# Splitting all weights on VectorE, and writing dense weights over expert weights block by block

## The chip, the cores and the metric

The kernel runs on one core of a Trainium2 chip. The metric is the device time of one execution, in microseconds (us). A core has five engines, each with a queue of its own that it works off in order: TensorE (PE: matmuls, with PEld for its weight loads), VectorE (DVE), ScalarE (ACT), GpSimd (POOL) and SyncE (SP, which issues DMAs). Engines wait for one another through semaphores only.

## What is computed

A two-layer "macaron" network on x of shape (4, 256, 256), that is 1024 tokens of width 256. `_L0_ffn` is a mixture of 16 experts of width 176 (4 per token) with a shared expert of width 704; `_L1_ffn` is a mixture of 32 experts of width 96 (up to 8 per token), which the kernel computes densely for all tokens; `_L0_attn` is an attention with 16 heads; `_L1_attn` is a state-space layer.

```python
x = L0_attn_x
x = x + 0.5 * _L0_ffn_ref(_layernorm(x), ...)
x = x + _L0_attn_ref(_layernorm(x), ...)
x = x + 0.5 * _L0_ffn_ref(_layernorm(x), ...)
x = x + 0.5 * _L1_ffn_ref(_layernorm(x), ...)
x = x + _L1_attn_ref(_layernorm(x), ...)
x = x + 0.5 * _L1_ffn_ref(_layernorm(x), ...)
```

All inputs are float32. The kernel multiplies in float16 and keeps the precision by splitting each operand into a high half and a low half (`whi` and `wlo` of the weights, `xhi` and `xlo` of the input, `hhi` and `hlo` of the hidden layer) and adding three products: high by high, high by low, low by high.

## The kernel before

The 1024 tokens are two halves of 512. The feed-forward work is twelve passes (`PASSES`), numbered p0 to p11: a shared pass of 6 units (SH: p0, p2, p4, p6), a routed pass of 16 units (RT: p1, p3, p5, p7), each for one half and one of the two uses of `_L0_ffn`, and four dense passes of 24 units (F1: p8 to p11). A unit is `gate` and `up` (matmuls into PSUM), `tanh` (ScalarE), `act` (VectorE), `h` (VectorE), `hi` (ScalarE), `lo` (GpSimd, `hh` or `hp` minus its high half) and `down` (matmuls). A routed unit handles two blocks of 128 token slots, each block of one expert; the tokens are scattered to DRAM by `send` (GpSimd, indirect DMA), loaded transposed by `load_xs` (SyncE), the result goes through `turn`, `hT_copy`, `y_copy` and `store_y`, and is gathered back by `gather` (GpSimd) and `combine` (VectorE, L1475). A dense unit has one more VectorE step, `fac` (L1330), that multiplies by the routing factor of each token.

The order of the work is written out by hand: `make_threads` makes lists ("threads") of pieces for each engine, and the strings in `ORDER` say how the threads of one engine are merged, one letter a thread and a number for how many pieces. In the VectorE string `m` is `act`, `h` and `fac`, `w` the weights' low halves, `c` `combine`, `r` the routing, `A` to `D` the layer norm. The strings decide what stands in front of what on an engine; the waits in each `piece` decide when it runs.

Weights come in pieces through a ring of 12 slots (`SLOTS`) in the tile `stage`. The first `NW0` = 40 pieces are 6 shared ones (768 columns), 32 half experts (608 columns) and 2 of the attention (768); `load_w0` loads piece g into slot g % 12 once the low half of piece g - 12 is made. The 28 chunks of the dense stage and the state-space layer (`WCH1`, 768 columns) follow as pieces 40 to 67: `load_w1`. Each piece is split like this: ScalarE writes `whi` = 256 x stage as float16 (`w0_hi` L851, `w1_hi` L864). Then either VectorE makes `wlo` = 256 x stage - `whi` in one `scalar_tensor_tensor` (L1387; pieces 0 to 5 and the even ones up to 38, 23 in all), or ScalarE scales the stage in place (`w0_scale` L854, `w1_scale` L868) and GpSimd subtracts (`w0_lo` L766, `w1_lo` L771): the 17 odd pieces 7 to 39 and all 28 chunks.

The tiles `whi` and `wlo` hold shared weights, attention weights and experts; the dense chunks are written over them. Chunk 0 waits until the last shared pass (p6) is done, chunk 8 (`EXP0 // CW`), the first that reaches into expert columns, until the last routed pass (p7) is done:

```python
if n == 0:
    act.wait_ge(down_done, UNIT[6] + NSH)
if n == EXP0 // CW:
    act.wait_ge(down_done, UNIT[7] + NRT)
```

In the order of before, ScalarE has `w1_hi` 0 to 7 within p7 and 8 to 27 within the first 14 units of p8; GpSimd has `w1_lo` 0 to 7 after units 5 to 11 of p7, and 8 to 27 after units 1 to 21 of p8. Unit c of p8 waits for chunk c, the state-space layer's `proj` for chunk 27. Unit c of p1 waits for the experts up to 2c + 1 (`wait_expert`).

## Time and profile before

| | us |
|---|---|
| median of 3 runs | 994.18 |
| lowest, highest | 990.6, 996.01 |
| the profiled execution, its time | 983.99 |
| its span, first to last instruction | 982.2 |
| its mean granted clock of TensorE | 0.959 of full speed |

The profile is of one execution. Its page gives the busy time of each engine, the span in 40 slices and the costliest groups of instructions; the other views give busy time in chosen stretches, groups by line, and the instructions in order of time. "Idle before, released by" stands in square brackets behind an instruction in the timeline. Busy time is not the same as time on the path that sets the end.

### The profile page before, as it was taken

How to read it: one execution, taken by the hardware profiler on the slowest of the kernel's cores; microseconds unless marked ns; L12 is line 12 of the kernel's file. 1: busy time of each engine (PE TensorE's matmuls, PEld its weight loads, DVE VectorE, ACT ScalarE, POOL GpSimd, SP SyncE). 2: the span in 40 equal slices, each digit the busy share in tenths (PEclk: the TensorE clock that was granted, in tenths of full speed). 3: DMA queues.
4: the chain of work that ended last, by engine and by line, in shares of the span. 5: the costliest groups of instructions: out<-in, count | busy, mean ns of one | idle time of the engine just before them, and what ended most of it. 6: DMA issues, size and time to landing. Idle time of an engine off the chain costs nothing.

```text
span 982.2 us, 20723 instructions
## 1 busy us (share of the span) xinstructions
PE 855.6 (87%) x6872; PEld 557.1 (57%) x6872; DVE 712.4 (73%) x1392; ACT 500.0 (51%) x929; POOL 477.3 (49%) x464
## 2 busy tenths in 40 slices
PE   2767788999748899788889897899999899999997
PEld 1356666777424667647675554454566445665564
DVE  6897326988778888736447987888978777785554
ACT  2867553688515677536767852345333543333332
POOL 3865278424667344288825866532443224432322
PEclk9979999999559999999999998999999999999999
DMA  8796546632122224847965522111110211112221
GB/s 303 287 219 154 138 146 123 135 85 59 60 65 78 64 55 102 254 153 154 195 166 167 166 100 68 47 54 47 51 57 23 76 51 47 54 41 92 73 68 65
DMA packets 123267, 106.62 MB, mean 109 GB/s; under 512 B 75672, under 2 KB 97944, under 8 KB 123168
## 3 DMA queue, kind: packets, MB, share of 16 engines
q1 hardware_dynamic: 117024, 88.51, 32.1%
q0 software_dynamic: 6144, 16.79, 6.0%
q8 instruction: 62, 1.02, 0.4%
q14 instruction: 37, 0.30, 0.1%
HBM read 58.98 MB, written 30.02 MB: 91 GB/s over the span
## 4 chain that ended last, share of the span: by engine, by line
PE 60%; issue 7%; DVE 6%; POOL 3%; ACT 2%; DMA 2%; SPq 1%; POOLq 0%; DVEq 0%; ACTq 0%
PE ps L1063 24%; PE ps L1110 12%; PE ps L1038 7%; PE ps L1092 5%; PE ps L1254 2%; PE ps L1078 1%; PE ps L1177 1%; PE ps L1216 1%; PE ps L1211 1%; PE ps L1285 1%; DVE hid L1330 1%; DVE hid L1324 1%; POOL back L760 1%; PE ps L1274 1%; POOL xs_dram L745 1%
## 5 line engine op out<-in xcount | busy, mean ns | idle before, releaser
L717 POOL TENSOR_TENSOR hh<-hid,hh 128x512 f16<-128x512 f32 x120 | 143.5, 1198 | 238.7 <-ACT hh L829 238.4
L1324 DVE SCALAR_TENSOR_TENSOR hid<-gtanh,ps 128x512 f32<-128x512 f32 (+2 forms) x184 | 114.4, 622 | 160.4 <-ACT gtanh L808 145.8
L1063 PE MATMUL ps<-xhi,whi 128*128 128x512 f16 x480 | 186.8, 389 | 24.4 <-DVE hid L1324 20.1
L808 ACT ACTIVATE gtanh<-ps 128x512 f32<-128x512 f32 (+2 forms) x184 | 100.4, 545 | 204.7 <-PE ps L1063 169.3
L1063 PE MATMUL ps<-xlo,whi 128*128 128x512 f16 x480 | 186.5, 388 | 0.0
L1063 PE MATMUL ps<-xhi,wlo 128*128 128x512 f16 x480 | 186.1, 388 | 0.0
L1110 PE MATMUL ps<-whi,hh 128*128 128x256 f16 x960 | 174.5, 273 | 5.2 <-POOL hh L717 5.2
L1038 PE MATMUL ps<-whi,xs_sb 128*128 x992 | 130.5, 245 | 34.1 <-issue 23.6
L1338 DVE SCALAR_TENSOR_TENSOR hid<-hid,ps 128x512 f32<-128x512 f32 (+2 forms) x184 | 114.6, 623 | 28.9 <-PE ps L1038 12.2
L1110 PE MATMUL ps<-wlo,hh 128*128 128x256 f16 x480 | 131.0, 273 | 0.0
L829 ACT ACTIVATE hh<-hid 128x512 f16<-128x512 f32 x120 | 75.1, 626 | 95.1 <-DVE hid L1330 64.8
L1038 PE MATMUL ps<-wlo,xs_sb 128*128 x496 | 118.0, 242 | 0.0
L1110 PEld LDWEIGHTS ps<-whi,hh 128*128 128x128 f16 x960 | 94.1, 98 | 30.3 <-issue 5.9
L1038 PEld LDWEIGHTS ps<-whi,xs_sb 128*128 128x128 f16 x992 | 71.7, 99 | 55.9 <-issue 44.0
L714 POOL TENSOR_TENSOR hp<-hid,hp 128x352 f16<-128x352 f32 x64 | 57.0, 892 | 94.7 <-ACT hp L819 94.5
L1063 PEld LDWEIGHTS ps<-xhi,whi 128*128 128x128 f16 x480 | 47.8, 100 | 80.0 <-issue 33.1
L1330 DVE TENSOR_TENSOR hid<-hid,xs_sb 128x512 f32<-128x512 f32 x96 | 84.3, 878 | 9.8 <-DMA xs_sb<-c_dram 7.5
L1063 PEld LDWEIGHTS ps<-xhi,wlo 128*128 128x128 f16 x480 | 47.9, 100 | 59.8 <-issue 5.5
L745 POOL DMA_INDIRECT xs_dram<-xr,pos x64 | 65.9, 1030 | 28.3 <-issue 26.5
L1092 PE MATMUL ps<-whi,hh 128*128 x372 | 75.2, 282 | 4.4 <-ACT hh L836 3.7
L760 POOL DMA_INDIRECT back<-ys_dram,pos x64 | 68.5, 1070 | 16.4 <-issue 14.7
L1063 PEld LDWEIGHTS ps<-xlo,whi 128*128 128x128 f16 x480 | 47.8, 100 | 44.5 <-issue 3.9
(208 smaller groups left out, 1587.4 us busy)
## 6 DMA issues: line engine op xcount, KB each, us to landing
ys_dram<-y_sb SPq DMA_DIRECT2D x60, 256.0 KB, 2.5
xs_sb<-c_dram SPq DMA_DIRECT2D x64, 192.0 KB, 2.7
scr<-w_in SPq DMA_DIRECT2D x28, 384.0 KB, 4.9
scr<-we_in SPq DMA_DIRECT2D x32, 304.0 KB, 4.6
xs_sb<-c_dram SPq DMA_DIRECT2D x64, 128.0 KB, 2.9
xs_sb<-c_dram SPq DMA_DIRECT2D x64, 64.0 KB, 2.7
xs_dram<-y_sb SPq DMA_DIRECT2D x1, 3968.0 KB, 15.0
scr<-ws_in SPq DMA_DIRECT2D x8, 384.0 KB, 7.1
```

Source lines behind the costliest of these rows:

```text
L717: pool.tensor_tensor(hlo[:, k, :], hid[:, k % 2, :], hhi[:, k, :], ALU.subtract).then_inc(lo_done, 1)
L745: pool.indirect_dma_start(out=xs_dram, out_offset=bass.IndirectOffsetOnAxis(ap=pos[:, h, j, i:i + 1], axis=0), in_=xr[:, i, :], in_offset= ...
L760: pool.indirect_dma_start(out=back[:, slot, :], out_offset=None, in_=ys_dram[h], in_offset=bass.IndirectOffsetOnAxis(ap=pos[:, h, j, t:t + ...
L808: act.activation(gtanh[:, n % 2, 0:w], ps[:, G_BANK, 0:w], ACT.Tanh, scale=0.5 / W_SCALE)\
L829: act.activation(hhi[:, k, :], hid[:, k % 2, :], ACT.Copy).then_inc(hi_done, 1)
L1038: mm = pe.matmul(ps[:, bank, j * I0:(j + 1) * I0], xs_sb[:, slot + j, a + kc, :], w[:, ds(offset[k + j] + (EXP0 + kc * 2 * I0 + part), I0) ...
L1063: mm = pe.matmul(ps[:, bank, :], w[:, off:off + P], a[:, kc, t0:t0 + HN], start=(i == 0), stop=(i == 3 * KC - 1))
L1092: mm = pe.matmul(ps[:, Y_BANK + m % 2, D * b:D * b + D], hh[0:wide, k, at_h:at_h + P], w[0:wide, ds(offset[2 * (n % REGS) + b] + (EXP0 + 2 ...
L1110: mm = pe.matmul(acc[:, i, :], a[:, k, i * P:(i + 1) * P], w[:, off:off + D], start=(c == 0 and i % 2 == 0 and m == 0), stop=(c == NUM[r] ...
L1324: dve.scalar_tensor_tensor(out=hid[:, k, 0:w], in0=gtanh[:, k, 0:w], scalar=1.0, in1=ps[:, G_BANK, 0:w], op0=ALU.add, op1=ALU.mult).then_i ...
L1330: dve.tensor_tensor(hid[:, n % 2, :], hid[:, n % 2, :], fac[:, m % FRING, :], ALU.mult).then_inc(fac_done, 1)
L1338: dve.scalar_tensor_tensor(out=hid[:, k, 0:w], in0=hid[:, k, 0:w], scalar=scale, in1=ps[:, U_BANK, 0:w], op0=ALU.mult, op1=ALU.mult).then_ ...
```

## The change

All 45 pieces that GpSimd split are split by VectorE, with the same fused instruction as the others; the scalings of the stage on ScalarE and the subtractions on GpSimd go. A helper `w_split` names the semaphore and count of a piece, and every waiter uses it, `load_w0` and `load_w1` on SyncE among them. A dense chunk n that reaches into expert columns waits for only as many routed units of p7 as can still use these experts (`chunk_free`: an expert has at most four blocks, so block b is never of an expert below b // 4; chunk 9 waits for 4 units, 12 for 8, 15 for 12, 19 and later ones for 16). The lower bound of the expert's offset in `gate` says the same to the compiler. The strings of `ORDER` are written anew for all five engines.

```diff
@@ -220,7 +220,7 @@
         put("ACT", "w", "w0_hi", g)
-        if g < NSH or g % 2 == 0:
+        if g < NW0:
             put("DVE", "w", "w0_lo", g)
@@ -231,8 +231,7 @@
         put("ACT", "w", "w1_hi", j)
-        put("ACT", "w", "w1_scale", j)
-        put("POOL", "w", "w1_lo", j)
+        put("DVE", "w", "w1_lo", j)
@@ -560,13 +559,20 @@
-            return g < NSH or g % 2 == 0
+            return True
 
         def lo_count(g):
 
-            if g >= NW0:
-                return lo_count(NW0 - 1) + g - NW0 + 1
             return sum(piece_on_dve(i) == piece_on_dve(g) for i in range(g + 1))
+
+        def w_split(g):
+
+            return (w_lo_dve if piece_on_dve(g) else w_lo_pool), lo_count(g)
+
+        def chunk_free(n):
+
+            last = ((n + 1) * CW - 1 - EXP0) // EW
+            return (HN // P) * (last + 1) // 2
@@ -683,7 +686,7 @@
                     if n >= SLOTS:
-                        sp_.wait_ge(w_lo_pool, lo_count(g - SLOTS))
+                        sp_.wait_ge(*w_split(g - SLOTS))
@@ -764,11 +767,6 @@
-                elif name == "w1_lo":
-                    g = NW0 + n
-                    pool.wait_ge(w_scaled, lo_count(g))
-                    pool.tensor_tensor(wlo[:, n * CW:(n + 1) * CW], stage[:, g % SLOTS, :], whi[:, n * CW:(n + 1) * CW],
-                                       ALU.subtract).then_inc(w_lo_pool, 1)
@@ -859,14 +857,10 @@
-                    if n == EXP0 // CW:
-                        act.wait_ge(down_done, UNIT[7] + NRT)
+                    if n >= EXP0 // CW:
+                        act.wait_ge(down_done, UNIT[7] + min(NRT, chunk_free(n)))
...
-                elif name == "w1_scale":
-                    g = NW0 + n
-                    act.activation(stage[:, g % SLOTS, :], stage[:, g % SLOTS, :], ACT.Copy, scale=W_SCALE)\
-                        .then_inc(w_scaled, 1)
@@ -1022,7 +1016,8 @@
-                            offset[k + j] = pe.snap(at_expert[k + j], min_val=0, max_val=(E0 - 1) * EW)
+                            offset[k + j] = pe.snap(at_expert[k + j], min_val=(2 * c + j) // (HN // P) * EW,
+                                                        max_val=(E0 - 1) * EW)
@@ -1387,6 +1382,12 @@
+                elif name == "w1_lo":
+                    g = NW0 + n
+                    dve.wait_ge(w_hi, g + 1)
+                    dve.scalar_tensor_tensor(out=wlo[:, n * CW:(n + 1) * CW], in0=stage[:, g % SLOTS, :], scalar=W_SCALE,
+                                             in1=whi[:, n * CW:(n + 1) * CW], op0=ALU.mult, op1=ALU.subtract)\
+                        .then_inc(w_lo_dve, 1)
```

The new strings, read out as pieces:

| engine | before | after |
|---|---|---|
| PE | second half's `logits` before the gate of p1, unit 0; its `rank` before unit 3 | `logits` after the gate of p1, unit 11; `rank` after the gate of unit 12 |
| DVE | 13 of its 23 `wlo` pieces by the end of p0; routing of the second half within units 0 to 3 | pieces 0 to 19 before `act` of p1, unit 0; 20 to 36 before `h` of unit 5; routing of the second half in units 11 to 13 |
| DVE | no dense piece | `w1_lo` 0 to 15 behind `h` of p7, units 4 to 15; 16 to 21 behind p8, units 0 to 8; 22 to 27 from p8, unit 20 to p9, unit 1 |
| ACT | `w1_hi` 0 to 7 in p7 | `w1_hi` 0 to 15 in p7, chunk 12 behind the `y_copy` of unit 9; 16 to 27 in p8, units 0 to 6 |
| POOL | `send` of the first half with three `lo` and one `wlo` between | the same with two `lo` and no `wlo` between |
| SP | `load_w0` 0 to 22, then the first transposed load | `load_w0` 0 to 25, then the first three transposed loads |

## Rows read from the trace of the kernel before

**Rows 1.** The page: TensorE in 40 slices; the DMA view: transposed loads, us to landing.

```profile
PE   2767788999748899788889897899999899999997
...
xs_sb<-xs_dram SPq DMA_TRANSPOSE x124, 3.4
```

**Rows 2.** Busy time by stage: us, busy (count) per engine, clock, DMA share, GB/s.

```profile
20.00:62.60 42.60, 25.73 (x156) 13.30 (x156) 36.66 (x42) 29.66 (x48) 33.26 (x29) 0.92 0.82 281
62.60:90.00 27.40, 22.86 (x240) 20.13 (x241) 23.97 (x57) 22.15 (x44) 18.13 (x14) 0.88 0.83 180
90.00:135.00 45.00, 35.25 (x373) 28.58 (x373) 16.18 (x40) 24.55 (x56) 17.72 (x19) 0.96 0.52 134
...
450.00:515.00 65.00, 55.13 (x633) 45.05 (x631) 33.65 (x96) 46.22 (x95) 39.88 (x40) 1.00 0.76 174
515.00:650.00 135.00, 119.62 (x740) 70.03 (x738) 109.56 (x165) 66.97 (x109) 86.47 (x72) 0.96 0.34 105
650.00:982.00 332.00, 322.55 (x1971) 187.84 (x1970) 242.28 (x411) 122.92 (x205) 106.30 (x97) 0.99 0.18 57
```

**Rows 3.** Timeline, DVE, POOL, PE, 49 to 63 us: start, duration, idle before.

```profile
49.11 8.31 DVE L1387 SCALAR_TENSOR_TENSOR wlo<-scr,whi 128x608 f16<-128x608 f32 x1
...
50.44 3.94 POOL L766 TENSOR_TENSOR wlo<-scr,whi 128x608 f16<-128x608 f32 x3
...
60.71 0.19 PE L1146 MATMUL ps<-rwhi,xhi 128*128 128x32 f16 x1 [8.03 <-issue]
...
62.63 0.47 PE L1038 MATMUL ps<-whi,xs_sb 128*128 x2 [0.91 <-issue]
```

**Rows 4.** Timeline, POOL, DVE, PE, 594 to 604 us.

```profile
594.52 1.17 POOL L717 TENSOR_TENSOR hh<-hid,hh 128x512 f16<-128x512 f32 x1
...
598.35 3.22 POOL L771 TENSOR_TENSOR wlo<-scr,whi 128x768 f16<-128x768 f32 x2
...
594.79 7.07 DVE L1475 SCALAR_TENSOR_TENSOR x<-back,wk,x 128x256 f32<-128x256 f32 x1 [0.78 <-DMA back<-ys_dram,pos]
...
603.20 0.58 PE L1063 MATMUL ps<-xhi,whi 128*128 128x512 f16 x1 [5.46 <-DVE hid L1324]
```

**Rows 5.** Dense stage by shape, 515 to 650 us: busy us, mean ns, idle before.

```profile
L1330 DVE TENSOR_TENSOR hid<-hid,xs_sb 128x512 f32<-128x512 f32 x27 | 34.3, 1271 | 3.3 <-DMA xs_sb<-c_dram 2.6
...
L1475 DVE SCALAR_TENSOR_TENSOR x<-back,wk,x 128x256 f32<-128x256 f32 x16 | 19.3, 1234 | 0.8 <-DMA back<-ys_dram,pos 0.8
L1324 DVE SCALAR_TENSOR_TENSOR hid<-gtanh,ps 128x512 f32<-128x512 f32 x28 | 19.1, 684 | 13.9 <-ACT gtanh L808 13.7
```

**Rows 6.** Weight lines: ns min/median/max, first and last start, forms.

```profile
L1387 DVE SCALAR_TENSOR_TENSOR wlo<-scr,whi x23: 779/951/8315, 21.9 to 98.3; 128x608 f16<-128x608 f32 x16, 128x768 f16<-128x768 f32 x7
...
L766 POOL TENSOR_TENSOR wlo<-scr,whi x17: 1325/1357/1880, 41.5 to 105.9; 128x608 f16<-128x608 f32 x16, 128x768 f16<-128x768 f32 x1
...
L771 POOL TENSOR_TENSOR wlo<-scr,whi x28: 1627/1646/2080, 472.6 to 625.0; 128x768 f16<-128x768 f32 x28
...
L868 ACT ACTIVATE scr<-scr x28: 826/832/845, 455.3 to 581.5; 128x768 f32<-128x768 f32 x28
```

**Rows 7.** Timeline, POOL scatters of the first half (first, last), SP.

```profile
21.05 1.25 POOL L745 DMA_INDIRECT xs_dram<-xr,pos  x1 [5.37 <-issue]
...
46.98 1.04 POOL L745 DMA_INDIRECT xs_dram<-xr,pos  x1 [0.30 <-issue]
...
50.27 2.62 SPq L650 DMA_TRANSPOSE xs_sb<-xs_dram  x2
```

**Rows 8.** A routed block on TensorE: the chain at 176 us; timeline at 89.65 us.

```profile
178.57 0.91 PE ps L1038 x12
179.48 1.09 PE ps L1092 x10
...
182.53 0.33 PE ps L1078 x6
...
89.65 0.32 PE L1038 MATMUL ps<-whi,xs_sb 128*128 x2 [1.60 <-DVE wlo L1387]
```

More of the change, by code:

```diff
@@ L1006, in wait_shared @@
             def wait_shared(j):
-                pe.wait_ge(w_lo_dve, lo_count(j))
+                pe.wait_ge(*w_split(j))
             def wait_expert(e):
-                pe.wait_ge(w_lo_dve, lo_count(NSH + 2 * e))
-                pe.wait_ge(w_lo_pool, lo_count(NSH + 2 * e + 1))
+                pe.wait_ge(*w_split(NSH + 2 * e))
+                pe.wait_ge(*w_split(NSH + 2 * e + 1))
             def piece(name, n):
```

19 lines of the change are left out of this document (8 added, 11 removed), and 98 rows, old and new, of the table ORDER.

## The prediction

> **What bounds the kernel now.** I read the page first, then the busy time stage by stage, then the waits, and last the timeline of each engine around the gaps of TensorE. TensorE's slices are near nine tenths in most of the span [rows 1]; they show where it isn't at work: at the start, and twice in the middle. The stages put numbers on it [rows 2]. TensorE is idle for 42.6 - 25.73 = 16.9 us from 20 to 62.6 us (shared pass 0 and the first expert weights), 4.5 us to 90 us (first half of routed pass 1), 9.8 us to 135 us, 9.9 us from 450 to 515 us (routed pass 7), and 15.4 us from 515 to 650 us (dense pass 8, while the dense weights are still being split). After 650 us, when no weight is left to split, only 9.4 of 332 us are idle. So the time is TensorE's work plus its gaps, and a change to VectorE, ScalarE or GpSimd counts only where it closes or opens a gap.
>
> The gaps have one cause in common. A VectorE instruction with both inputs in SBUF that starts beside a run of GpSimd subtractions does not end before the run does. At 49.11 us the low half of an expert piece takes 8.31 us while GpSimd works off `hh` and `wlo` subtractions; TensorE, whose next instruction is the router's logits (they need a VectorE result queued behind), stands for 8.03 us [rows 3]. At 594.79 us one `combine` takes 7.07 us: GpSimd began a run of `hh` and `wlo` subtractions at 594.52 us and ended it at 601.57 us; TensorE's matmuls wait 5.46 us and start again at 0.58 us each, the slow rate [rows 4]. By shape, `fac` (L1330) has a mean of 1.27 us in this stage, where L1324, as wide but with an input in PSUM, has 0.684; `combine` (L1475), half as wide, has 1.23 us [rows 5]. The instructions that read PSUM do not stretch. That is 27 x (1.271 - 0.684) + 16 x (1.234 - 0.684) = 24.6 us of VectorE time at least, lost in this stage.
>
> **The change, part by part.** Removed: 17 + 28 = 45 GpSimd subtractions of 1.36 and 1.65 us (23.1 + 46.1 = 69 us), and 45 ScalarE scalings of about 0.7 and 0.83 us (L868 has the row of the wider; some 35 us). Added: 45 fused VectorE instructions, of which the 23 there are show the price: 16 at best 0.78 us for a 608-wide piece, 7 are 768 wide and take about the median of 0.95 us. That is 16 x 0.78 + 29 x 0.95 = 40.0 us [rows 6]. The price is known; the question is only what it stands beside.
>
> *Start, to 135 us.* The part that sets the first routed block is the scatter of the tokens: 16 indirect DMAs on GpSimd from 21.05 to 48.02 us, with three `lo` and one `wlo` subtraction between them, then the transposed loads, issued at 50.27 us and taking 2.62 us to issue [rows 7]. The new order takes out one `lo` (1.17 us [rows 4]) and the `wlo` (1.36 us [rows 6]): scatters end at 45.5 us, the pair of transposes is issued by 45.5 + 2.25 + 2.62 = 50.4 us, and lands 3.4 us later [rows 1], at 53.8 us. In the new order the gate of block 0 of pass 1 follows the shared pass at once and the logits of the second half come eleven blocks later, so the 8.03 us stall has nothing to stand on. VectorE must have made pieces 0 to 19 and twelve `act` and `h` by then: 6 x 0.95 + 14 x 0.78 + 12 x 0.684 = 25 us from 22 us on, plus some 4 us (an estimate: six small steps at most as long as an `act` each) for block table and layer norm: 51 us. I put the first routed gate at 55 us, a little behind the landing, in place of 62.63 [rows 3]: 7.6 us gained (bounds 3, if VectorE has all its pieces 5 us late, and 9, if it lands at once). Next, blocks 0 to 5 of pass 1. They take 89.65 - 62.63 = 27.0 us [rows 3, 8]. TensorE needs 2 x 0.91 + 1.09 + 0.33 = 3.24 us a block, 19.4 us for six. VectorE in the new order has 18 pieces there and twelve narrower `act` and `h`: 18 x 0.78 + 12 x at most 0.684 = 22.2 us, and about 2 us for the shared output's add. VectorE is the later one: 24 us, 3 us gained (bounds: loss of 3, gain of 7). From 90 to 135 us the y stores and the transposes set the pace and stay: 0 (-3 to +3). Start: 10.6 us gained.
>
> *New waits.* `w1_hi` from chunk 9 on waits for a number of routed blocks in place of all 16. Behind it on ScalarE stand `tanh`, `hi` and `y_copy` of later blocks, and TensorE behind these. But each such wait stands after a `y_copy` that waits for the same block or a later one (chunk 12 asks for 8 blocks and follows `y_copy` of the tenth), so it costs nothing. On SyncE `load_w0` and `load_w1` now wait for VectorE's pieces; behind them stand transposed loads and y stores. The piece waited for is 12 back: cover of several us, and if it is gone, each late piece costs TensorE its 0.78 to 0.95 us. Cost 0 (0 to 4).
>
> *Pass 7, 450 to 515 us.* VectorE gets 16 pieces, 15.2 us, and is busy 33.7 of 65 us now; ScalarE changes 8 scalings for 8 or 9 `w1_hi` of about the same length; GpSimd loses 13 us [rows 2, 6]. VectorE would be at 49 of 65 us, so it doesn't bind, but a piece in front of an `act` delays the chain gate, `tanh`, `act`, `up`, `h` of a block. Bounds: nothing, or half of the pieces on the path, 8 us, or a gain of 3 for transposes of `h` that wait less for GpSimd. I take a loss of 2.
>
> *Pass 8, 515 to 650 us.* VectorE gets the other 12 pieces (11.4 us) and loses the 24.6 us of stretching: 109.6 - 24.6 + 11.4 = 96 of 135 us [rows 2, 5, 6], so it is less loaded than before with more to do. What is left on GpSimd is one `lo` of 1.17 us [rows 4] per block, and there are 28 blocks in 135 us [rows 5], so a stretch ends after at most that. Of 15.4 us idle and some 4 us of slow clock (119.6 us busy at a granted clock of 0.96 in place of 1.00 [rows 2]) I leave 4 us for the routing and the factor loads: 15 us gained (bounds 6 and 19).
>
> Other stages hold no changed instruction, only another order: 0 (-5 to +5).
>
> Sum against the profiled execution (span 982.2, 983.99 us): -10.6 + 0 + 2 - 15 = -23.6, so 960.4 us. The runs shown have a median of 994.18, 10.2 us more than the profiled one; I take the difference over: 970.6 us.
>
> How a stretch ends can be set against a page. The stretched `combine` spans four GpSimd instructions [rows 4]. The Trainium skill, page "SBUF — State Buffer", section "SBUF: two separate sides", says that whichever engine starts first has the shared ports for its one whole instruction. By that, a stretch is at most one subtraction, 1.65 us, and the new VectorE instructions, with two SBUF inputs, would hold up GpSimd's `lo` in turn. The trace shows the run, not the one instruction, as the unit, so the rule alone undersells what goes away.
>
> **Rivals.** *VectorE is late.* In pass 1 and pass 7 it takes its upper costs: the six blocks get 3 us longer in place of 3 shorter, pass 7 loses 8 in place of 2. Then the sum is -7.6 + 3 + 8 - 15 = -11.6: 982.6 us. For it: its work per block in pass 1 is above TensorE's. Against: the stage from 90 us leaves VectorE idle for 29 of 45 us [rows 2], so a delay there is made good.
>
> *An overlap costs one instruction's length only.* The removed pieces then explain 1.65 of the 8.03 us and 1.65 of the 5.46 us, 0.2 to 0.3 of a gap. With 0.3 of the 25.6 us gained, less 2: -5.7, 988.5 us. Against: the `combine` and the run of four subtractions end within 0.3 us of each other [rows 4]. The rule of that page would end here.
>
> *More closes than I count.* All bounds of the gain together are 17 us more; some two thirds of that, because GpSimd's `lo` and ScalarE are free earlier: 960 us.
>
> *The gap only changes its owner*: TensorE waits for the y stores, the scatters and the routing of the second half, and the end stays, 994 us. For it: the start is full of such transfers (DMA share 0.82 and 0.83 [rows 2]).
>
> *Slower.* VectorE's pieces lie on the path in all three stages. Place: between `act` and `h` of one block, where the new order puts up to three pieces. Price: 40.0 us if each piece delays TensorE by its length, less the 25.6 recovered: +14.4, 1008.6 us. It decides once more than 25.6 of the 40 us, two pieces in three, lie on the path; against it, VectorE has 24 us of work to TensorE's 19.4 in six blocks of pass 1, and room in passes 7 and 8.
>
> **How the numbers follow.** Forecast 0.55 (970.6 us), VectorE late 0.13 (982.6), one instruction only 0.07 (988.5), more closes 0.10 (960), gap changes owner 0.08 (994), slower 0.07 (1008.6). The range leaves out the last two, and takes in the rest with some room below for the bounds of the unchanged stages: 954 to 988 us. A measurement of this kernel tells about 0.5% from no change, 5 us: below 989.2 is faster, 0.82 (of the one-instruction case about half); within, 0.11; above 999.2, 0.07.
>
> **What would show it.** Right: no GpSimd `wlo`; L1330 and L1475 near 0.69 and 0.5 us on average; first routed gate near 55 us; TensorE idle under 6 us in pass 8; first dense chunk beyond the eighth split before the last routed block. Wrong: VectorE's `wlo` as the releaser of TensorE's waits in pass 1 or 7; `fac` still stretched beside single `lo`; a new gap at the routing of the second half.

## The result, and the profile after

| | before | after |
|---|---|---|
| median of the runs, us | 993.52 (990.6 to 996.01, 4 runs) | 951.08 (944.98 to 952.91, 4 runs) |
| profiled execution, us (span) | 983.99 (982.2) | 952.91 (951.1) |
| granted clock of that execution | 0.959 | 0.973 |

The ratio is 0.9563, 95% interval 0.9509 to 0.9617: 43 us faster. Forecast were 970.6 us and a range of 954 to 988 us; 951.08 lies below it. The direction was right, the size was not: 43 us where 23.6 were summed.

The first view of after is the busy time by stage, as in [rows 2]: the start, pass 1 up to 79 us (its block 6 begins on TensorE at 81.27 us), the rest of pass 1, pass 7, pass 8, and the rest. Columns are us, busy us (instructions) of PE, PEld, DVE, ACT, POOL, then clock, DMA share and GB/s.

```profile
20.00:55.60 35.60, 28.09 (x155) 15.62 (x156) 27.15 (x41) 25.91 (x42) 25.23 (x22) 0.95 0.84 313
55.60:79.00 23.40, 17.73 (x201) 14.14 (x199) 19.78 (x36) 16.83 (x34) 6.24 (x6) 1.00 1.07 252
79.00:128.00 49.00, 40.08 (x455) 31.60 (x454) 26.69 (x81) 26.24 (x59) 18.19 (x19) 1.00 0.55 131
...
438.00:508.00 70.00, 58.47 (x639) 46.09 (x637) 50.12 (x112) 47.35 (x97) 28.09 (x32) 0.98 0.86 197
508.00:603.00 95.00, 94.96 (x620) 57.84 (x619) 80.23 (x145) 40.11 (x70) 48.47 (x43) 1.00 0.39 114
603.00:951.00 348.00, 340.06 (x2085) 199.32 (x2083) 259.45 (x444) 129.59 (x215) 116.03 (x105) 1.00 0.19 57
```

In pass 8 TensorE is busy for 94.96 of 95.00 us at a clock of 1.00. It has no gap left. At the start there is still one (28.09 of 35.60 us), and in pass 7 another (58.47 of 70).

The same pass of before, cut at its own ends, shows what its 117.5 us were made of: 15.4 us idle (117.50 - 102.12), and 7.0 us by which TensorE was busy longer than the 95.16 us that after needs for the same matmuls.

```profile
516.20:633.70 117.50, 102.12 (x632) 59.36 (x630) 97.07 (x134) 60.94 (x98) 79.58 (x63) 0.96 0.35 108
```

The lower clock is only a part of these 7.0 us. The granted clock was 0.72 from 566 to 572 us and 0.66 from 600 to 610 us, behind the two long gaps, and 1.00 elsewhere: 0.28 x 6 + 0.34 x 10 = 5.1 us at most, gaps included. What the other 2 us are no row shows.

The shapes of pass 8 on VectorE answer to [rows 5] (busy us, mean ns, idle before):

```profile
L1325 DVE TENSOR_TENSOR hid<-hid,xs_sb 128x512 f32<-128x512 f32 x24 | 19.9, 830 | 0.8
...
L1388 DVE SCALAR_TENSOR_TENSOR wlo<-scr,whi 128x768 f16<-128x768 f32 x12 | 14.1, 1183 | 0.0
L1476 DVE SCALAR_TENSOR_TENSOR x<-back,wk,x 128x256 f32<-128x256 f32 x16 | 7.7, 532 | 0.0
```

`fac` fell from a mean of 1.271 to 0.830 us, `combine` from 1.234 to 0.532. The new pieces of VectorE cost what the old ones did (minimum, median, maximum in ns, first and last start), none of them above 2 us:

```profile
L1382 DVE SCALAR_TENSOR_TENSOR wlo<-scr,whi x40: 778/784/1744, 21.8 to 95.4; 128x608 f16<-128x608 f32 x32, 128x768 f16<-128x768 f32 x8
...
L1388 DVE SCALAR_TENSOR_TENSOR wlo<-scr,whi x28: 944/951/1926, 455.7 to 606.9; 128x768 f16<-128x768 f32 x28
```

At the start, the timeline answers to [rows 3, 7]: the last of the first half's scatters on GpSimd, the transposed loads on SyncE's queue, the first gate of pass 1 on TensorE, which waited for nothing.

```profile
44.10 0.98 POOL L748 DMA_INDIRECT xs_dram<-xr,pos  x1 [0.31 <-issue]
...
47.63 7.86 SPq L653 DMA_TRANSPOSE xs_sb<-xs_dram  x6
...
54.53 0.31 PE L1033 MATMUL ps<-whi,xs_sb 128*128 x2
```

To see where the 31 us between the two profiled executions are, take the first `tanh` of each pass on ScalarE as its begin:

```
begin of          before   after   lead
pass 1              64.6    55.6    9.0
pass 2             137.3   128.0    9.2
pass 7             449.1   438.0   11.1
pass 8             516.2   507.7    8.5
pass 9             633.7   602.9   30.8
end                982.2   951.1   31.1
```

Pass 8 gave 22.3 us, the start 9, and all the rest nothing on balance. Blocks 0 to 5 of pass 1 gave next to nothing: block 6 begins on TensorE at 81.27 us, 26.7 us behind the first gate, where before took 27.0, and what it waited for is a VectorE piece:

```profile
81.27 0.32 PE L1033 MATMUL ps<-whi,xs_sb 128*128 x2 [0.76 <-DVE wlo L1382]
```

The medians differ by 12 us more than these two executions do; that is a question of its own below.

### The profile page after: what moved, and what is told of

It reads as the page before. It is cut to its first block, busy times and chain, and to the rows that moved or that the text cites. A ratio compares the mean times of both kernels' runs of the same rounds, so it can differ in the third digit from the quotient of the medians.

```text
span 951.1 us, 20697 instructions
## 1 busy us (share of the span) xinstructions
PE 845.6 (89%) x6872; PEld 554.0 (58%) x6872; DVE 704.3 (74%) x1437; ACT 469.5 (49%) x884; POOL 416.1 (44%) x419
## 4 chain that ended last, share of the span: by engine, by line
PE 73%; issue 7%; DVE 5%; POOL 4%; DMA 4%; another core or an unknown queue 2%; SPq 2%; ACT 2%; POOLq 0%; DVEq 0%; ACTq 0%
PE ps L1058 29%; PE ps L1105 15%; PE ps L1033 10%; PE ps L1087 6%; POOL xs_dram L748 3%; PE ps L1249 2%; PE ps L1073 2%; PE ps L1172 2%; DMA xs_dram<-y_sb 2%; DMA scr<-we_in 1%; PE ps L1211 1%; PE ps L1206 1%; PE ps L1280 1%; SPq L653 1%
## 5 line engine op out<-in xcount | busy, mean ns | idle before, releaser
L1105 PE MATMUL ps<-whi,hh 128*128 128x256 f16 x960 | 176.8, 275 | 7.2 <-POOL hh L720 7.2
L717 POOL TENSOR_TENSOR hp<-hid,hp 128x352 f16<-128x352 f32 x64 | 59.6, 932 | 125.7 <-ACT hp L817 125.4
L1325 DVE TENSOR_TENSOR hid<-hid,xs_sb 128x512 f32<-128x512 f32 x96 | 71.6, 746 | 5.5 <-DMA xs_sb<-c_dram 3.0
L1087 PE MATMUL ps<-whi,hh 128*128 x372 | 72.5, 275 | 2.6 <-ACT hh L834 2.5
## 6 DMA issues: line engine op xcount, KB each, us to landing
xs_sb<-c_dram SPq DMA_DIRECT2D x64, 128.0 KB
```

The source lines that it names most:

```text
L1087: mm = pe.matmul(ps[:, Y_BANK + m % 2, D * b:D * b + D], hh[0:wide, k, at_h:at_h + P], w[0:wide, ds(offset[2 * (n % REGS) + b] + (EXP0 + 2 ...
L1105: mm = pe.matmul(acc[:, i, :], a[:, k, i * P:(i + 1) * P], w[:, off:off + D], start=(c == 0 and i % 2 == 0 and m == 0), stop=(c == NUM[r] ...
L1325: dve.tensor_tensor(hid[:, n % 2, :], hid[:, n % 2, :], fac[:, m % FRING, :], ALU.mult).then_inc(fac_done, 1)
```

## The experiments

Blocks are named pass.block. Each run has its own runs of the kernel before on the same chip, so ratios can be compared from chip to chip (after: 0.956) and microseconds of pass 8 and of the start too (pass 9 took 123.0 to 123.4 us in every profile); the lengths of pass 1 and of passes 2 to 6 only on one chip.

### Does GpSimd's subtraction make pass 8 long?

Twenty subtractions are put back beside the changed kernel, as ballast. In the next three runs the ballast lies on scratch columns that, as it turned out, hold the head constants of the last stage, so that stage computes with overwritten constants; its instructions are the same.

```diff
   pool.tensor_tensor(hlo[:, k, :], hid[:, k % 2, :], hhi[:, k, :], ALU.subtract).then_inc(lo_done, 1)
+  for _ in range({1: 1, 2: 1, 4: 1, 5: 1, 7: 1, 9: 1, 10: 1, 11: 1, 12: 1, 13: 1, 14: 1, 16: 1, 17: 2,
+                  18: 1, 19: 2, 20: 2, 21: 1}.get(c, 0) if r == F1_PASSES[0] else 0):
...
+      pool.tensor_tensor(scr[:, 10368 + 384 * (k % 4):10752 + 384 * (k % 4)].bitcast(F16),
+                         scr[:, 9216:9984], scr[:, 9984:10368].bitcast(F16), ALU.subtract)
```

> The changed kernel with 20 more GpSimd subtractions in pass 8, each 768 wide (float32 minus float16 into float16, as the removed ones of the dense chunks), on scratch columns that nobody reads, behind the lo of the blocks where the kernel before had its own. No engine waits for them; they change nothing of the output. Theory (GpSimd's reads stretch VectorE's instructions with two SBUF inputs, and that was the time of pass 8): fac in pass 8 goes from a mean of 0.75 us back to 1.1 to 1.3 us, pass 8 from 95.2 to 103 to 115 us, the whole to 959 to 971 us. Rival 1 (pass 8 gained from the dense weights being written early, or from ScalarE's removed scalings): fac may stretch, but pass 8 stays within 2 us of 95.2 and the whole at 951. Rival 2 (an overlap costs one instruction's length only): fac near 0.95 us, pass 8 at most 97 us.

Measured: pass 8 took 113.5 us (+18.3), the ratio is 0.9703 (0.9671 to 0.9734). On that chip the kernel before took 982.37 us and passes 2 to 6 were shorter in every profile, so the whole, 951.63 us, says less than pass 8 does; by its ratio it is 14 us longer than after. VectorE and TensorE in pass 8:

```profile
L1333 DVE TENSOR_TENSOR hid<-hid,xs_sb 128x512 f32<-128x512 f32 x24 | 30.0, 1252 | 0.8
...
L1341 DVE SCALAR_TENSOR_TENSOR hid<-hid,ps 128x512 f32<-128x512 f32 x24 | 16.4, 685 | 0.7
L1327 DVE SCALAR_TENSOR_TENSOR hid<-gtanh,ps 128x512 f32<-128x512 f32 x24 | 16.3, 679 | 9.9 <-POOL hh L721 8.8 <-ACT gtanh L814 1.1
...
PE ps L1066 <- DVE hid L1327: 12.7, 10, 2.4
```

`fac` is back at 1.252 us, the two that read PSUM stay at 0.685 and 0.679, and TensorE waits ten times for `act` (L1327). But see what `act` itself waited for: 8.8 us for GpSimd's `hh` (L721), the `lo` that the ballast had pushed back (3.4 us in after). `combine` is not back: a mean of 0.568 us, where before had 1.234. So two mechanisms work here, the stretch and GpSimd's own lateness.

The same ballast in five runs of four:

```diff
-  for _ in range({1: 1, 2: 1, 4: 1, 5: 1, 7: 1, 9: 1, 10: 1, 11: 1, 12: 1, 13: 1, 14: 1, 16: 1, 17: 2,
-                  18: 1, 19: 2, 20: 2, 21: 1}.get(c, 0) if r == F1_PASSES[0] else 0):
+  for _ in range({3: 4, 7: 4, 11: 4, 15: 4, 19: 4}.get(c, 0) if r == F1_PASSES[0] else 0):
```

> The same 20 subtractions, but in five runs of four, behind the lo of blocks 3, 7, 11, 15 and 19 of pass 8. If a VectorE instruction stays blocked to the end of a run of back-to-back GpSimd instructions, single fac or combine of 5 to 8 us appear, about one a run, TensorE stands about 4 us at each, and pass 8 gets 15 to 25 us longer (110 to 120 us), more than with the same work laid singly. If only one instruction's length is lost at a time, no fac is longer than 1.6 + 0.7 = 2.3 us or so and pass 8 is no longer than with single ones. If nothing of this is on the path, 95 us.

Measured: pass 8 at 122.8 us (+27.6), ratio 0.9809 (0.9768 to 0.985). The same work in runs costs 9 us more than laid singly. One `fac` was shut out for the whole run; in another run a `wlo` was not (timeline, DVE and POOL):

```profile
550.46 7.62 DVE L1333 TENSOR_TENSOR hid<-hid,xs_sb 128x512 f32<-128x512 f32 x1
...
551.11 6.42 POOL L728 TENSOR_TENSOR scr<-scr 128x768 f16<-128x768 f32 x4
...
509.01 2.40 DVE L1396 SCALAR_TENSOR_TENSOR wlo<-scr,whi 128x768 f16<-128x768 f32 x1
...
506.82 7.69 POOL L728 TENSOR_TENSOR scr<-scr 128x768 f16<-128x768 f32 x4
```

`fac` ended at 558.08 us, 0.55 us behind the end of the run at 557.53. The `wlo` that began at 509.01 us, in the middle of the other run, ended at 511.41, while that run went on to 514.51; there GpSimd paid, 7.69 us for four in place of 6.42. The five runs took 7.69, 7.27, 6.42, 6.95 and 8.05 us, so the run that shut VectorE out is the shortest. Forecast were about five such long stops; there was one, and pass 8 is longer than forecast all the same, since GpSimd's `lo` stands behind each run as well.

The control: GpSimd writes but reads nothing.

```diff
-      pool.tensor_tensor(scr[:, 10368 + 384 * (k % 4):10752 + 384 * (k % 4)].bitcast(F16),
-                         scr[:, 9216:9984], scr[:, 9984:10368].bitcast(F16), ALU.subtract)
+      pool.memset(scr[:, 9216 + 768 * (k % 4):9984 + 768 * (k % 4)].bitcast(F16), 0.0)
```

> The changed kernel with 20 GpSimd memsets of 1536 float16 columns in the places of the 20 subtractions: GpSimd writes SBUF but reads nothing. If it is GpSimd's reading that stretches VectorE, fac stays at 0.75 us and pass 8 at 95 us. If any GpSimd work does (or if it only matters that GpSimd's own lo comes later), fac and pass 8 move as with the subtractions, in proportion to the memsets' own length, which no row shows yet.

```profile
L1333 DVE TENSOR_TENSOR hid<-hid,xs_sb 128x512 f32<-128x512 f32 x24 | 17.9, 746 | 0.8
...
L728 POOL MEMSET scr<- 128x1536 f16 x20 | 27.4, 1379 | 0.0
```

`fac` is not stretched (0.746 us) beside 27.4 us of memsets, yet pass 8 takes 101.3 us (+6.1), and `act` waits 6.6 us for GpSimd's `hh`. That is mostly the second mechanism, but not alone: some VectorE instructions with one SBUF tensor as input are held up by memsets. One that takes 0.18 us in the changed kernel took 2.60 us, to the end of a run of two (timeline, DVE and POOL):

```profile
565.69 2.60 DVE L1505 TENSOR_SCALAR active<-cum 128x28 f32<-128x28 f32 x1
...
565.56 2.69 POOL L728 MEMSET scr<- 128x1536 f16 x2
```

Of the 18.3 us of the subtractions, then, at most some 6 to 7 are GpSimd's lateness (the memsets are 1.38 us long, the subtractions 1.61 at their fastest) and some 11 to 12 the stretch. This split is an estimate; it takes the two to add up.

ScalarE's removed scalings, put back as ballast (scratch columns that no stage uses):

```diff
   act.activation(whi[:, n * CW:(n + 1) * CW], stage[:, g % SLOTS, :], ACT.Copy, scale=W_SCALE).then_inc(w_hi, 1)
+  act.activation(scr[:, s:s + 6 * P].rearrange("p (a b) -> p a b", b=P),
+                 ident.unsqueeze(1).to_broadcast([P, 6, P]), ACT.Copy, scale=W_SCALE)
```

> The changed kernel with 45 more ScalarE copies with a scale, of 640 and 768 columns, one behind the high half of each piece that had a scaling before; they read a constant and write scratch columns that nobody reads, and nobody waits for them. They test the rival that the removed 35 us of ScalarE work were part of the gain. Expected: at most 0.8 us at a few blocks of pass 1 and pass 7, pass 8 at 95 to 97 us, the whole within 4 us of the changed kernel (ratio to before 0.955 to 0.960). If the scalings mattered: 4 us or more.

Measured: 953.94 us, ratio 0.9621 (0.9575 to 0.9668). Pass 8 took 98.6 us, +3.3 where at most 1.8 were expected, and pass 2 began at 129.4 us (126.9 and 128.0 in the two profiles of after). The whole is some 6 us longer by its ratio, where at most 4 were expected; with two runs the intervals still overlap. So ScalarE's part of the split is a term too, which the prediction had set to nothing, and every gain of "moved work" below has it inside.

### Undoing one part, doing one part

Dense chunks back on ScalarE and GpSimd, behind the same blocks, with the early writing kept:

```diff
-        put("DVE", "w", "w1_lo", j)
+        put("ACT", "w", "w1_scale", j)
+        put("POOL", "w", "w1_lo", j)
```

> One part of the change undone: the 28 dense chunks have their low halves from ScalarE's scaling and a GpSimd subtraction again, behind the same blocks as VectorE's pieces stand now; the expert pieces stay on VectorE, and the early writing of the dense weights stays. Theory: the start keeps its gain (first block of pass 6 within 2 us of 409), pass 8 is 10 to 18 us longer than 95.2, pass 7 within 3 us, and the whole is 962 to 972 us. If the early writing is what made pass 8 shorter, the whole stays within 3 us of 951.

Measured: ratio 0.9661 (0.9631 to 0.9691), pass 8 at 105.2 us (+10.0, the low edge of what was expected), pass 7 at 71.3, the start as in after (pass 1 at 56.2 us). Pass 8 held 13 of these subtractions, not 20: the early writing had put the others into pass 7.

Odd expert pieces back on GpSimd, in the new order:

```diff
-        if g < NW0:
+        if g < NSH or g % 2 == 0:
             put("DVE", "w", "w0_lo", g)
```

> Another part undone: the 17 odd expert and attention pieces have their low halves from ScalarE's scaling and a GpSimd subtraction again, in the new order, behind the same blocks; the dense chunks stay on VectorE. If these subtractions delayed the scatters and stretched VectorE at the start, the first block of pass 1 moves from 55.6 to between 58 and 65 us and the whole is 3 to 9 us longer than the changed kernel. If the start's gain came from the new order alone (logits of the second half eleven blocks later), the first block of pass 1 stays at 55 to 57 us and the whole within 2 us. Pass 8 stays at 95 us in both cases.

Measured: ratio 0.9694 (0.9643 to 0.9745). On one chip with `after_again`, pass 1 began at 62.4 us in place of 55.7 and pass 2 at 139.8 in place of 126.9: 12.8 us, more than the 9 expected; from there on nothing (the ends differ by 13.3), and pass 8 was 95.2 us. TensorE waited for GpSimd, and VectorE was held up beside `hh` and two `wlo` (waits of TensorE from 20 to 140 us: us, times, longest; timeline of DVE and POOL):

```profile
PE ps L1031 <- POOL wlo L767: 8.4, 4, 3.2
...
38.34 4.78 DVE L1380 SCALAR_TENSOR_TENSOR wlo<-scr,whi 128x608 f16<-128x608 f32 x1
...
39.81 2.65 POOL L767 TENSOR_TENSOR wlo<-scr,whi 128x608 f16<-128x608 f32 x2
```

Late writing again, once in an order close to that of before, once laid out evenly:

```diff
-                        act.wait_ge(down_done, UNIT[7] + min(NRT, chunk_free(n)))
+                        act.wait_ge(down_done, UNIT[7] + NRT)
```

> The third part undone: chunks 8 to 27 of the dense weights are written only after the last routed block of pass 7, as in the kernel before, with ScalarE's, VectorE's and SyncE's orders moved accordingly; all low halves stay on VectorE. Theory (pass 8 gained from GpSimd's missing subtractions): 20 pieces of 0.95 us stand in pass 8 in place of 12, VectorE has room, pass 7 gets up to 3 us shorter and pass 8 up to 4 us longer: whole within 3 us of the changed kernel. Rival (the early writing is the gain): pass 8 at 108 to 118 us, the whole 12 to 20 us longer.

> The changed kernel with chunks 8 to 27 written only after pass 7 once more, but laid out one a block: in the run before, two VectorE pieces stood ahead of a block's act and waited 3.6 us for ScalarE, which cost pass 8 5.8 us at one block; that was the order and not the late writing. Here ScalarE's part of a chunk comes four blocks and VectorE's three blocks ahead of its use. Theory (early writing is worth little by itself once GpSimd has no subtractions): pass 8 at 95 to 99 us, the whole within 4 us of the changed kernel. Rival (late writing costs in any order): pass 8 at 104 us or more.

Measured: ratios 0.9692 (0.9633 to 0.9751) and 0.9653 (0.9602 to 0.9704); pass 8 at 106.7 and 102.5 us, pass 7 at 70.9 and 71.0. Neither side's figures came out: theory had pass 8 at most at 99 us, the rival at 108 and at 104 us or more. The theory that late writing costs nothing once GpSimd is free is wrong: in the better of two layouts it costs 7.3 us of pass 8. Twenty pieces then stand in a pass in which TensorE needs 3.9 us a block and VectorE was busy for 80 of 95 us with twelve. An order tuned for it might do better; 7.3 us is an upper bound.

One part alone, in the order of before. First the dense chunks:

```diff
-        put("ACT", "w", "w1_scale", j)
-        put("POOL", "w", "w1_lo", j)
+        put("DVE", "w", "w1_lo", j)
```

> The kernel before with one part of the change alone: the 28 dense chunks have their low halves from one fused VectorE instruction, behind the same blocks where GpSimd had them; no early writing, every other order as before, expert pieces still half on GpSimd. Theory (the subtractions on GpSimd were what pass 8 lost): pass 8 goes from 117.5 to 98 to 104 us, pass 7 within 2 us, the whole 12 to 20 us faster than before. Rival, after the run with late writes (106.7 us in pass 8 with all low halves on VectorE): the early writing is worth 11 us of its own, so pass 8 stays at 106 us or more and the whole gains 11 us or less.

Then the odd expert pieces:

```diff
-            return g < NSH or g % 2 == 0
+            return g < NW0
```

> The kernel before with only the 17 odd expert and attention pieces moved from GpSimd to VectorE, each behind its even neighbour; all other orders as before (the logits of the second half still stand early in pass 1), dense chunks still on GpSimd. If the subtractions themselves cost the start (stretching and late scatters), the first block of pass 1 goes from 64.7 to 56 to 60 us, pass 2 begins 8 to 13 us earlier, and the whole is 6 to 13 us faster than before. If the gain needs the new order, the first block of pass 1 stays above 62 us and the whole gains 3 us or less; if VectorE is then late in pass 1, pass 1 gets longer than 75 us and it may be slower.

Measured: ratios of 0.9936 (0.9917 to 0.9956) for the chunks and 0.9983 (0.9952 to 1.0013) for the expert pieces. The chunks alone gave 6.3 us where 12 to 20 were expected, the expert pieces nothing. Undone, the same parts cost 10 and 13 us by their ratios. In pass 8 with the chunks on VectorE (111.4 us) the rows show who is late now (waits: us, times, longest):

```profile
PE ps L1049 <- DVE hid L1310: 9.9, 5, 2.7
PEld ps L1049 <- DVE wlo L1379: 8.9, 4, 3.1
```

And at the start, with the expert pieces on VectorE, the 8.03 us stall of [rows 3] is 2.56 us long, but it ends no earlier (62.03 us, 60.71 in [rows 3]). VectorE, which owes the logits their operand, itself stood for ScalarE's high half before (timelines of TensorE and of VectorE):

```profile
62.03 0.18 PE L1143 MATMUL ps<-rwhi,xhi 128*128 128x32 f16 x1 [2.56 <-issue]
63.93 0.32 PE L1035 MATMUL ps<-whi,xs_sb 128*128 x2 [0.95 <-issue]
```

```profile
57.96 0.79 DVE L1384 SCALAR_TENSOR_TENSOR wlo<-scr,whi 128x608 f16<-128x608 f32 x1 [2.96 <-ACT whi L848]
```

### The corners: moved work without the order, order without the moved work

The kernel before with all 45 pieces on VectorE, every order and wait as it was:

```diff
-            return g < NSH or g % 2 == 0
+            return True
```

> All 45 pieces moved to VectorE's fused operation, but every order and wait as in the kernel before (a piece stands behind its even neighbour, a chunk behind the block where GpSimd had it), late writing too. If the parts add up as they did alone (0.4 and 6.3 us): 5 to 9 us faster than before, pass 8 at 109 to 113 us, first block of pass 1 at 65 to 67 us. If the moved work is what counts and the two parts only hid each other: 15 us or more faster. If the new order is what makes room for VectorE's pieces: under 10 us.

The changed kernel, new order and early writing, with the 17 and the 28 pieces on GpSimd:

```diff
-            return True
+            return g < NSH or (g < NW0 and g % 2 == 0)
```

> The other corner: the new order and the early writing, with the 17 expert pieces and the 28 dense chunks on ScalarE and GpSimd as before. If the costs of undoing add up (13.3 and 9.6 us): 23 us slower than the changed kernel, so 18 to 22 us faster than before (ratio about 0.98), pass 1 beginning at 62 us and pass 8 at 103 to 107 us. If the order without the moved work is worth nothing: ratio 0.995 to 1.005. If the order is the whole gain it would be at 0.956, which the two runs before speak against.

Ratios and, from the profiles, the begin of pass 2 and the length of pass 8:

```
                              ratio (95%)                pass 2 begins   pass 8
old order, GpSimd's half      1                          137.3, 140.3    117.5
old order, all on VectorE     0.988  (0.9822 to 0.9939)  140.0           110.6
new order, GpSimd's half      0.9783 (0.9727 to 0.9838)  142.3           102.8
new order, all on VectorE     0.9559 (0.9508 to 0.961)   128.0, 126.9     95.2
```

In pass 8 the two add up: 6.9 us from the moved work, 14.7 from the order with the early writing, 22.3 together. At the start they do not: each alone gains nothing at the begin of pass 2, together some 9 to 13 us. The two middle rows are of one chip, on which the changed kernel with one place put back (the last two runs of this section) began pass 2 at 128.1 and 128.5 us. By its ratio `before_all_dve` is 12 us faster (6 to 18), between the 5 to 9 us expected if the parts add and the 15 or more if the moved work is what counts; the ratio alone can't tell these apart, the begin of pass 2 does. In pass 8 of `before_all_dve` no instruction is stretched much (`fac` has a mean of 0.765 us, in `all_on_gpsimd` 0.934), and it is still the longer of the two:

```profile
L1316 DVE TENSOR_TENSOR hid<-hid,xs_sb 128x512 f32<-128x512 f32 x24 | 18.4, 765 | 2.8 <-DMA xs_sb<-c_dram 2.2
...
L1335 DVE TENSOR_TENSOR hid<-hid,xs_sb 128x512 f32<-128x512 f32 x24 | 22.4, 934 | 2.4 <-DMA xs_sb<-c_dram 1.7
```

The start alone: the kernel before with the 17 pieces on VectorE and the new order of all engines up to block 2.0, from there the old one:

```diff
-        if g < NSH or g % 2 == 0:
+        if g < NW0:
             put("DVE", "w", "w0_lo", g)
```

> The kernel before with the change in passes 0 and 1 alone: the 17 odd pieces on VectorE and the new order of all engines until the first block of pass 2; from there all is as before, the dense chunks on GpSimd too. Alone, the moved pieces had moved the begin of pass 2 by nothing (140.6 us) and the new order by nothing (142.3 us with GpSimd's half kept, against 137.3 and 140.3 us before). If the two gain only together: pass 1 begins at 55 to 57 us, pass 2 at 126 to 130 us, and the whole is 10 to 14 us faster than before (ratio 0.986 to 0.990). If part of the start's gain is given back in the old order of the later passes: under 8 us.

Measured: ratio 0.9845 (0.978 to 0.9909), 15.4 us of 995.24 (9 to 22), a little over the 10 to 14 expected; pass 1 began at 56.1 us, pass 2 at 129.6. That is the interaction shown directly, and it carries through the old order behind it.

One place of the order at a time, in the changed kernel. The last routing of pass 8, put back, written out for TensorE and for one step on VectorE (`route_keep`, `route_weights`, `route_exp`, `c_turn`, `c_copy` and `store_c` moved with them):

```diff
 PE  gate 8.17
-PE  logits 5
 PE  up 8.17
...
 PE  up 8.21
+PE  logits 5
...
 DVE act 8.17
-DVE route_top 5
 DVE h 8.17
...
 DVE h 8.21
+DVE route_top 5
```

> The changed kernel with one place of the order put back: the logits, the choice and the weights of the last routing in pass 8 stand at blocks 21 to 23 as in the kernel before, in place of blocks 17 to 20, on all four engines that take part. In the kernel before, block 22 took 10.1 us in place of 3.9 and with the chunks on VectorE still 7.7 us. If the place (routing steps between act and h of a block, with fewer down products of TensorE left to cover them) is what cost there, pass 8 goes from 95.2 to 98 to 102 us and the whole is 3 to 7 us longer. If only GpSimd's subtractions made it long, pass 8 stays within 1 us of 95.2; late pieces w1_lo 24 to 27 beside it could add 1 to 2 us.

Measured: pass 8 at 99.2 us (+4.0), ratio 0.9578 (0.9523 to 0.9634). Block 22, 3.9 us long in after and 10.1 in before, took 6.8, the next one 5.1. The place costs in pass 8, as expected; by its ratio the whole is 2 us longer, where 3 to 7 were expected. The logits of the second half, put back:

```diff
 PE  down 0.4
+PE  logits 1
 PE  gate 1.0
...
 PE  gate 1.11
-PE  logits 1
...
 DVE h 0.3
+DVE ln_lo 2
...
 DVE h 0.5
+DVE ln_lo 3
...
 DVE h 1.6
-DVE ln_lo 2
-DVE ln_lo 3
```

> The changed kernel with the other place put back: the logits of the second half, and the layer-norm halves on VectorE that they need, stand before block 0 of pass 1 as in the kernel before, in place of eleven blocks later. The prediction took this place for the 8.03 us stall. If the stall came from GpSimd's run holding VectorE alone, the logits find their operand ready: the first block of pass 1 stays within 1 us of 55.7 us and the whole within 2 us. If the place itself costs (TensorE waits at the logits for layer-norm work that stands behind VectorE's pieces), the first block of pass 1 moves to 58 to 62 us and the whole is 2 to 6 us longer.

Measured: the first block of pass 1 began at 58.2 us (+2.5, the place does cost there), pass 2 at 128.5, and the whole has a ratio of 0.9552 (0.9494 to 0.961): nothing is left of it at the end. So this place is not what the start's gain hangs on, and which place of the start's order is stays open.

### The twelve microseconds between profile and median

> The changed kernel unaltered, once more, as the measure for the others on the same chip, and to see how far one profiled execution stands from the median. The profiled runs told of 31 us between the two kernels, the medians of 43. If pass 8 is 95 us again and the experiments with added GpSimd work are right about the price of it, the whole is 930 to 940 us where the kernel before takes 982. If the difference of 43 us is the right one, 936 to 942 us; if 31 us is, 948 to 953 us.

> The kernel before unaltered. The question is the 10.2 us by which its profiled execution stood under the median of its runs. If that was a draw of the granted clock in stages that the change does not touch, this profile falls within 5 us of its median with other lengths of passes 2 to 6 (attention), and the same pass 8 of 117 us. If profiling itself makes the kernel before faster, it lies 8 us or more under the median again.

Measured: after_again 950.49 us (948.11 to 952.44), profiled 948.11; before_again 997.07 (993.88 to 1005.28, 10 runs), profiled 996.66. (The microseconds expected of the first were those of another chip; the difference by its ratio is 43.9 us.) So profiling does not make the kernel before faster: the first profile was a low draw. Against it this one is 12.7 us longer (994.9 to 982.2), 3.0 of it by pass 2, 5.1 in pass 6, 2.0 in pass 7. In pass 6 TensorE stood once, where the first profile shows no such gap:

```profile
436.89 0.39 PE L1092 MATMUL ps<-whi,hh 128*128 x1 [5.23 <-ACT hh L836]
```

What made ScalarE late there the profile does not name. This run is also a measure of the noise: the kernel before set against itself has a ratio of 1.0034 (1.0001 to 1.0066), so a difference of some 3 us can appear between equal kernels, and an interval that just misses 1 is weak evidence. On this chip the two kernels are 48.6 us apart: 9.2 by pass 1, 4.2 in pass 1, 10.0 in passes 2 to 6, 1.3 in pass 7, 22.3 in pass 8, 1.7 behind it. Passes 2 to 6 split no weight. They took 311.7 to 318.1 us in the profiles with the old order there (six, start_only's among them) and 304.1 to 310.2 in those with the new one on the same chips. The order alone: the kernel before, in which all five engines follow the new order from block 2.0 to block 7.0, with the weight pieces where they were. Two places of it on VectorE:

```diff
 DVE act 3.0
+DVE h 3.0
 DVE combine 2
-DVE h 3.0
 DVE act 3.1
+DVE h 3.1
 DVE combine 3
 DVE ln_stats 4
-DVE h 3.1
```

> The kernel before, with every piece of weight work as it was (GpSimd's half too, late writing too) and the orders of before in passes 0 and 1 and from pass 7 on; between the first block of pass 2 and the first block of pass 7 (attention and the routed pass behind it) the five engines follow the new order. No weight is split in that stretch, so no moved work is in it. In the profiles so far this stretch takes 311.7 to 318.1 us in five runs with the old order and 304.0 to 310.2 us in the runs with the new one. If that is the order: the stretch takes 304 to 310 us here and the whole is 4 to 9 us faster than before (ratio 0.991 to 0.996). If it comes from elsewhere (what the earlier passes leave behind, the clock): 311 us or more, and the whole within 2 us of before.

Measured: ratio 0.9946 (0.9913 to 0.9979), so 5.4 us (2 to 9); passes 2 to 6 took 310.1 us, the edge of what was expected; one profile of before has 311.9. It began later (pass 2 at 144.3 us), so a part of the shorter stretch may be only that. The ratio speaks for the order, but weakly, beside the 3 us above; where in the five passes the gain sits is not shown.

The parts come close to the whole: 15.4 (start_only) + 5.4 (order_mid) + 22.3 (pass 8) = 43.1 us, against 43 to 44 measured. The first term has an interval of some 6 us to each side, and the third is read from profiles, so the sum is no proof.

## Why the prediction was right and wrong

*What bounds the kernel: right.* TensorE's gaps, closed one by one, are the gain, and in pass 8 all of it: the 15.4 us idle and the 7.0 us of longer busy time went to nothing. *That the gaps have one cause in common: wrong.* The stretch beside GpSimd's runs is one of several, as the terms below show.

*Start, -7.6: right in size, wrong in cause.* Pass 1 began 9.0 us earlier, its first gate 8.1. The chain of scatters came out as worked out: the last one ended at 45.08 us (forecast 45.5), the issue of the transposes began at 47.63 (forecast 45.5 + 2.25 = 47.75), the first gate started at 54.53 (forecast 55). But the prediction let the moved pieces and the new order each have a share. Either alone brings nothing to the begin of pass 2 (140.6, 140.0 and 142.3 us). With the old order VectorE has the pieces, and its wait for ScalarE, on the way to the logits; with the new one and GpSimd's pieces, TensorE waits for GpSimd. The late one only changes its name, the rival "the gap changes its owner", and it took both edits to be rid of it. The 8.03 us stall was read rightly as VectorE held up, but it lay beside a second lateness of nearly its length, so shortening it (to 2.56 us) gave nothing.

*Six blocks of pass 1, -3: did not come.* They gained 0.3 us (27.0 to 26.7), and by the `tanh` begins 0.5 us in the second pair and a loss of 0.5 in the first. VectorE's work was to take 24 us; TensorE waited 6.0 us for `act` in pass 1, and for a `wlo` once. *90 to 135 us, 0:* the rest of pass 1 gained 0.8 us in the first pair of profiles and 3.7 in the second, about the bound of 3.

*New waits, 0: right.* SyncE waited 1.3 us for VectorE's pieces in pass 7, within the bound of 4 us. What the wait of `w1_hi` allows was not priced at all: writing the dense chunks early is worth up to 7.3 us, because it takes eight pieces out of pass 8. The prediction counted those eight in pass 7 (as 16 and 12) and did not ask what 12 in place of 20 do for pass 8.

*Pass 7, +2: within its bounds.* 2.6 us longer in one pair, 1.3 shorter in the other.

*Pass 8, -15: the term that was mis-sized, 22.3.* Two steps failed. "I leave 4 us for the routing and the factor loads" left what the new order takes away: the routing four blocks earlier is 4.0 us of it. And beside the 15.4 us idle only "some 4 us of slow clock" were counted, where TensorE's busy time for the same matmuls shrank by 7.0. The clock itself was priced about right (5.1 us at most); the other 2 us appear only when the busy times at both ends are set side by side. As to the cause, the removed stretch, on which all 15 us were laid, is a third of the 22.3 us or so: the moved work gives 6.9 us in the old order and 7.6 to 10.0 in the new, GpSimd's lateness and ScalarE's scalings included. The rest is the order with its early writing, of which two places are priced: the routing, 4.0, and the early writing, up to 7.3. The stretch of 24.6 us of VectorE time was real, and VectorE's time is not TensorE's: in the old order most of it only laid bare the next waits, for VectorE's own pieces (8.9 us of weight loads) and for the `act` behind them (9.9 us).

*Other stages, 0 (-5 to +5): low by some 5.4 us.* "Another order" was priced at nothing because no instruction changed. The width was about right, the middle was not.

*Profile to median, +10.2: the second large miss.* The step "I take the difference over" treats the distance of one execution from its median as a property of the kernel. It was a draw. The changed kernel's profiled execution lies at 952.91 us, 1.8 us above its median. With the term left out the forecast would have been 960.4; with the term, but with the 31.1 us by which the profiled executions differ, 963.1. Only both together come to the profiled 952.9: 984.0 - 31.1. Between the medians the term drops out, and the 19.5 us that the forecast lacks lie in the stages: 7.3 in pass 8, most of the rest in pass 1 and passes 2 to 6, which differ from pair to pair.

*What would show it.* No GpSimd `wlo`; `combine` 0.532 us (forecast 0.5); first gate 54.53 (55); TensorE idle 0.04 us in pass 8 (under 6): right. `fac` came to 0.830, not 0.69. Of the signs of being wrong, VectorE's `wlo` released TensorE for 0.8 us in pass 1 and not in pass 7 (the 6.1 us that it has besides are the first piece of pass 0), and single `lo` still stretch `fac`, to 1.606 us at most.

*How a stretch ends.* The trace of before showed one `combine` shut out by a run of four, and the prediction took the run for the unit. With 20 more subtractions in the kernel both kinds occur: one `fac` for 7.62 us over a run of four, four more for 2.86 to 3.39 us over `lo` and one subtraction, and six `wlo` for 2.38 to 2.40, one of them in the middle of a run of four. The Trainium skill, page "SBUF — State Buffer", section "SBUF: two separate sides", has the shared ports locked for one whole instruction, which fits the 2.4 us and the longer run of GpSimd (7.69 for 6.42) where VectorE got in between; for the 7.62 us it does not say why VectorE, already waiting, got no turn between four instructions. Neither the rule nor my reading holds alone. The rival built on that rule forecast 988.5 us by keeping most of the stretch; it fell because the stretch was not where most of the gain lay.

The same page, section "Who interferes with whom", sets apart a GpSimd instruction that only writes from one that reads. The memset run agrees for VectorE instructions with two SBUF inputs: `fac` 0.746 us beside 27.4 us of memsets.

## What to carry to other kernels

Moving work off an engine and reordering the instructions around it are to be priced as one: here neither alone made pass 2 begin earlier, and both together made it begin 9 to 13 us earlier. When a wait is closed, name the next one in the same stretch and its length; if it is nearly as long, the first is worth nothing by itself. Take a stage's recoverable time as the difference between its length and TensorE's busy time for the same matmuls in a stretch without gaps (here 117.5 - 95.2 us, all of it recovered), hold no allowance back for what the new order may remove as well, and never carry one execution's distance from the median over to another kernel.

## What the runs showed of the hardware

- A VectorE instruction with two SBUF inputs can be shut out for a whole run of GpSimd subtractions (7.62 us over a run of 6.42), or let in after the one that is running (2.40 us, and the run of four then takes 7.69). Why the one or the other happens the profiles do not tell.
- VectorE instructions with an input in PSUM were never touched: means of 0.679 to 0.688 us in pass 8 of every run shown, with 20 subtractions beside them or with none.
- GpSimd memsets of 1.38 us did not stretch `fac` (0.746 us) and hardly the `wlo` (0.975 us), but held up a VectorE instruction with one SBUF tensor as input, 2.60 us for 0.18. Pass 8 grew by 6.1 us, for the most part, it seems, since GpSimd's own `lo` came later behind them (`act` waited 6.6 us for it, 3.4 without them).
- The same kernel varied by 12.7 us between two profiled executions (982.2 and 994.9) with pass 8 at 117.5 us in both, its gaps included: 11.3 us of it lie before pass 8, 1.4 behind.
